# Attention stage: the row maximum from two GpSimd products and a VectorE maximum, instead of two clipped copies and three GpSimd instructions

## The reference, cut to what matters

```python
Q = (x @ Wq + bq).reshape(b, s, H, C) * inv_sqrt_c        # H = 16, C = 64
K = (x @ Wk + bk).reshape(b, s, H, C)
V = (x @ Wv + bv).reshape(b, s, H, C)
scores = jnp.einsum('bshq,bshk->bshqk', Q, K)             # an outer product per head
mask = jnp.triu(jnp.ones((C, C), dtype=bool), 1)
scores = jnp.where(mask, -jnp.inf, scores)
w = jax.nn.softmax(scores, axis=-1)
attn = jnp.einsum('bshqk,bshk->bshq', w, V)
out = attn.reshape(b, s, HID) @ Wo + bo
```

## Time and profile before

| what | value |
|---|---|
| median of the three runs | 3987.61 us |
| the profiled execution, its own time | 3990.44 us |
| its span in the profile | 3988.7 us |
| TensorE busy, share of the span | 3543.9 us, 89% |
| VectorE busy | 3277.2 us, 82% |
| ScalarE busy | 1974.6 us, 50% |
| GpSimd busy | 3341.5 us, 84% |
| L1249 (subtract, GpSimd), 768 instructions | 2509.0 us |
| chain that ended last, by engine | GpSimd 34%, TensorE 21%, issue 15%, VectorE 3% |

### The profile page before, as it was taken

One profiled execution on the slowest core, in us unless ns is written; L12 is line 12 of the kernel. 1 busy time (PEld: TensorE's weight loads), 2 busy tenths in 40 slices (PEclk: granted clock), 3 DMA queues, 4 the chain that ended last, 5 costly groups with the idle time before them and its releaser, 6 DMA issues.

```text
span 3988.7 us, 72222 instructions
## 1 busy us (share of the span) xinstructions
PE 3543.9 (89%) x25866; PEld 3108.7 (78%) x26059; DVE 3277.2 (82%) x3459; ACT 1974.6 (50%) x2535; POOL 3341.5 (84%) x1502
## 2 busy tenths in 40 slices
PE   5593699977699999999999999999999999999999
PEld 4252588866488888888888888888888888888888
DVE  8536555547699998899999999998999999999988
ACT  1010233344266655655555556555555555565555
POOL 1678455541699999999999999999999999999997
PEclk8696899998799999999999999999999999999999
DMA  9322456669000000000000000000000000000000
GB/s 381 109 101 80 140 178 197 187 210 339 14 5 5 8 5 5 5 5 5 5 5 6 6 5 8 5 5 5 5 5 6 5 5 6 5 8 5 5 5 5
DMA packets 110620, 209.18 MB, mean 52 GB/s; under 512 B 16608, under 2 KB 77280, under 8 KB 110304
## 3 DMA queue, kind: packets, MB, share of 16 engines
q1 hardware_dynamic: 84192, 140.90, 10.8%
q0 software_dynamic: 21504, 59.93, 4.1%
q10 hardware_dynamic: 4608, 4.20, 0.3%
HBM read 183.34 MB, written 107.74 MB: 73 GB/s over the span
## 4 chain that ended last, share of the span: by engine, by line
POOL 34%; PE 21%; issue 15%; DVE 3%; ACT 1%; another core or an unknown queue 0%; POOLq 0%; DVEq 0%; ACTq 0%
POOL at_s L1249 31%; PE at_num L1483 8%; PE at_den L1483 7%; PE at_work L1460 3%; PE at_work L1470 1%; POOL at_m L1234 1%; POOL at_fall L1231 1%; DVE at_pv L1167 1%; DVE at_k_low L1395 1%; PE at_misc L1515 1%; DVE at_s L1167 1%; PE at_misc L1509 1%; ACT at_s L1328 1%; DVE at_k_top L1392 0%; DVE at_pv L1168 0%
## 5 line engine op out<-in xcount | busy, mean ns | idle before, releaser
L1249 POOL TENSOR_TENSOR at_s<-at_s,at_m 128x2048 f32<-128x2048 f32 (+7 forms) x768 | 2509.0, 3303 | 34.9 <-DVE at_s L1167 25.4
L1328 ACT ACTIVATE at_s<-at_s 128x2048 f32<-128x2048 f32 (+7 forms) x768 | 1081.8, 1420 | 607.5 <-POOL at_s L1249 606.9
L1483 PE MATMUL at_den<-k_ident,at_s 128*128 128x128 f32 (+2 forms) x9216 | 1136.5, 273 | 50.3 <-ACT at_s L1328 50.3
L1483 PE MATMUL at_num<-k_ident,at_pv 128*128 128x128 f32 (+2 forms) x9216 | 1144.0, 274 | 14.0 <-issue 4.2
L1483 PEld LDWEIGHTS at_num<-k_ident,at_pv 128*128 128x128 f32 (+2 forms) x9216 | 1044.5, 141 | 90.7 <-issue 69.2
L1483 PEld LDWEIGHTS at_den<-k_ident,at_s 128*128 128x128 f32 (+2 forms) x9216 | 1031.8, 139 | 83.0 <-ACT at_s L1328 59.2
L1168 DVE TENSOR_TENSOR at_pv<-at_s,at_vp 128x2048 f32<-128x2048 f32 (+7 forms) x512 | 690.5, 1349 | 228.2 <-ACT at_vp L1303 174.6
L1168 DVE TENSOR_TENSOR at_s<-at_q,at_kp 128x2048 f32<-128x2048 f32 (+7 forms) x512 | 689.8, 1348 | 16.0 <-ACT at_kp L1298 11.2
L1167 DVE TENSOR_TENSOR at_pv<-at_s,at_vp 128x2048 f32<-128x2048 f32 x256 | 583.9, 2281 | 0.0
L1167 DVE TENSOR_TENSOR at_s<-at_q,at_kp 128x2048 f32<-128x2048 f32 x256 | 581.2, 2270 | 0.0
L1460 PE MATMUL at_work<-k_region,at_xT 128*128 128x512 f32 x788 | 409.8, 646 | 104.1 <-ACT at_k_far L1269 81.7
(11 more groups left out here) (235 smaller groups left out, 3475.6 us busy)
## 6 DMA issues: line engine op xcount, KB each, us to landing
moe_w<-experts SPq DMA_DIRECT2D x256, 384.0 KB
slot_x<-k_region SPq DMA_DIRECT2D x16, 2144.0 KB, 25.2
moe_x<-slot_x SPq DMA_DIRECT2D x256, 134.0 KB, 2.7
cmb_y<-picked SPq DMA_DIRECT2D x32, 768.0 KB, 7.7
at_xT<-xT SPq DMA_DIRECT2D x33, 128.0 KB, 2.1
e_x<-u SPq DMA_DIRECT2D x4, 1024.0 KB, 9.4
picked<-moe_yo,moe_row POOLq DMA_INDIRECT x256, 3.1
xT<-cmb_xT ACTq DMA_DIRECT2D x32, 128.0 KB, 5.9
```

Source lines behind the costliest of these rows:

```text
L1249: nc.gpsimd.tensor_tensor(part(s_slot, c), part(s_slot, c), by_query(m[unit_of(c)][:], c), ALU.subtract).then_inc(sub_done, 1)
L1328: nc.scalar.activation(part(s_slot, c), part(s_slot, c), ACT.Exp, scale=C ** -0.5).then_inc(exp_done, 1)
L1483: ins = nc.tensor.matmul(dst[0:wide, b * P:(b + 1) * P], buf[:, at:at + wide], k.ident[:], start=(c in (0, NTRI) and x == 0 and b == 0), s ...
```

## The change

`keep_q` now only copies q, and tells the others at once. GpSimd makes two products with q itself (`rise`): fall = k_low * q and m = k_top * q, behind its chunks 2 and 3 (unit 1) and behind chunks 20 and 21 (unit 0 of the next tile; the first of them stands ahead of `gated`). The third instruction goes to VectorE (`maxima`): m = max(m, fall), at its chunk 0 for unit 0 and at its chunk 6 for unit 1, behind that chunk's product, its `times_v` and its `divide`. Both inputs of this maximum lie in SBUF. The semaphore `max_step` becomes two, `risen` and `max_done`.

```diff
-                    if step == 0:
                         pool.wait_ge(scanned, t * 4 + 4)
                         pool.wait_ge(q_out, n + 1)
-                        nc.gpsimd.tensor_tensor(rows(m[h], FRONT), turned(k_top), rows(m[h], FRONT), ALU.mult).then_inc(max_step, 1)
-                    elif step == 1:
-                        nc.gpsimd.tensor_tensor(rows(fall), turned(k_low), rows(fall), ALU.mult).then_inc(max_step, 1)
+                        wait(pool, max_done, n)
+                        nc.gpsimd.tensor_tensor(rows(fall), turned(k_low), rows(q[h], FRONT), ALU.mult).then_inc(risen, 1)
                     else:
-                        pool.wait_ge(max_step, n * 3 + 2)
-                        nc.gpsimd.tensor_tensor(m[h][:, FRONT:QL], m[h][:, FRONT:QL], fall[:], ALU.subtract
-                                                ).then_inc(max_step, 1)
+                        wait(pool, sub_done, (t - 1) * NCH + (NCH if h else NTRI))
+                        nc.gpsimd.tensor_tensor(rows(m[h], FRONT), turned(k_top), rows(q[h], FRONT), ALU.mult).then_inc(risen, 1)
...
-                MAXIMA_HERE, MAXIMA_NEXT = {2: 0, 3: 1, 4: 2}, {21: 0, 22: 1, 23: 2}
+                RISE_HERE, RISE_NEXT = {2: 0, 3: 1}, {20: 0, 21: 1}
...
                         if c in (0, NTRI):
-                            pool.wait_ge(max_step, t * 6 + (3 + 3 * unit_of(c)))
+                            pool.wait_ge(max_done, t * 2 + (1 + unit_of(c)))
...
-                    nc.scalar.copy(q[h][:, FRONT:QL], work[:])
-                    wait(act, sub_done, past)
-                    nc.scalar.activation(m[h][:, FRONT:QL], work[:], ACT.Relu)
-                    wait(act, max_step, n * 3)
-                    nc.scalar.activation(fall[:], work[:], ACT.Relu, scale=-1.0).then_inc(q_out, 1)
+                    wait(act, risen, n * 2 - 2)
+                    nc.scalar.copy(q[h][:, FRONT:QL], work[:]).then_inc(q_out, 1)
...
-                        wait(dve, max_step, t * 6)
+                        wait(dve, risen, t * 4)
...
+                def maxima(t, h):
+                    n = t * 2 + h
+                    dve.wait_ge(risen, n * 2 + 2)
+                    v.tensor_tensor(m[h][:, FRONT:QL], m[h][:, FRONT:QL], fall[:], ALU.max).then_inc(max_done, 1)
...
+                MAXIMA_NEAR, MAXIMA_FAR = 0, 6
...
+                        if c == MAXIMA_NEAR:
+                            maxima(t, 0)
+                        if c == MAXIMA_FAR:
+                            maxima(t, 1)
```

More of the change, by code:

```diff
@@ L1099, in attention_and_ffn @@
         xT_in = [a.sem(f"xT_in{u}") for u in range(2)]
-        work_done, k_out, q_out, v_out, up_out, scanned, max_step = (
-            a.sem(s) for s in ("work_done", "k_out", "q_out", "v_out", "up_out", "scanned", "max_step"))
+        work_done, k_out, q_out, v_out, up_out, scanned, risen, max_done = (
+            a.sem(s) for s in ("work_done", "k_out", "q_out", "v_out", "up_out", "scanned", "risen", "max_done"))
         kp_ready, vp_ready, mult_done, sub_done, exp_done, pv_done = (
@@ L1220, in _, with rise @@
             def _(pool):
-                def maxima(t, h, step):
+                def rise(t, h, step):
                     n = t * 2 + h
@@ L1250, in tile @@
                                                 ALU.subtract).then_inc(sub_done, 1)
[L1251 to L1254, removed]
+                        if c in RISE_HERE:
+                            rise(t, 1, RISE_HERE[c])
+                        if c in RISE_NEXT:
+                            rise(t + 1, 0, RISE_NEXT[c])
                         if c == GATED:
                             gated(t)
-                for step in range(3):
-                    maxima(0, 0, step)
+                for step in range(2):
+                    rise(0, 0, step)
                 tile_loop(pool, tile)
```

## The result

| | kernel before | changed kernel |
|---|---|---|
| median of 20 runs each | 3987.64 us | 3995.23 us |
| lowest to highest | 3983.95 to 3992.97 | 3987.08 to 4009.30 |
| profiled execution, its own time | 3990.44 us | 4009.30 us |
| its span | 3988.7 us | 4007.5 us |

The ratio is 1.0019, 95% interval 1.0012 to 1.0027: 7.6 us slower, where +16 us was forecast. The sign was right, the size was not, and the changed kernel's runs spread over 22 us where those of before spread over 9. The profiled execution is the slowest of the 20, so I read its tiles one by one rather than its total.

The account below looks back on a forecast made before the run. A ring of waits through VectorE, TensorE and ScalarE was taken to bound the kernel. +0.39 us a tile gave +12 in 30 tiles, with +5 for the clock and -1 at the start +16: about 4004 us, range 3968 to 4020.

Parts of the forecast that it names:

- The ring of 42.04 + 47.33 + 2.45 us: Legs from VectorE's start to TensorE's V1, to ScalarE's copy of q, back to VectorE: the whole 91.82 us tile.
- GpSimd's 2.57 us of removed work: Two GpSimd instructions fewer a tile, outside the ring of waits: claimed to be worth nothing by itself.
- ScalarE, -0.96: Between the copy of Q1 and exp(1): without the two relus, vp comes 0.96 us earlier in the ring.
- VectorE, +0.60: The far maximum behind chunk 6 pushes VectorE's next instruction back by 0.60 us, covered by no idle time.
- The collision, +0.75: At the far maximum, VectorE waits 0.75 us for the rest of GpSimd's chunk 5 subtraction; chance 0.50.
- the main case: VectorE's far maximum waits only for the rest of GpSimd's running instruction: 3998 to 4016 us, chance 0.50.
- The ring, +0.39: Net change of the ring of waits, -0.96 + 0.60 + 0.75 = +0.39 us a tile, +12 us in 30 tiles.
- The clock, +5: TensorE's clock falls: if all 30 tiles pay 1.58 us instead of 24, +9 us; half taken, +5.
- the rival with chunk 6 ahead: GpSimd's chunk 6 goes ahead of the waiting far maximum, a 2.0 us wait: 3990 to 4037 us, chance 0.10.
- The sum: All terms together: +16 us on the profiled execution's 3990.44, so 4006.4, median about 4004; slower with chance 0.57.
- Second case (GpSimd lets VectorE in): The far maximum isn't held: -0.36 us a tile, faster, 3969 to 3977 us, chance 0.27.

Follow-up runs that it names:

- r4: The kernel before with VectorE's two K1 scans one chunk earlier, behind chunks 11 and 12: 3911.39 us, ratio 0.9805.
- r7: The changed kernel with two unread ScalarE relus put back behind each copy of q: 4007.29 us, ratio 1.0052.
- r1: The changed kernel timed and profiled again, unaltered: 3999.28 us, ratio 1.0035.
- r5: The kernel before plus an unread VectorE maximum behind chunks 0 and 6, one input in SBUF and one in PSUM: 3975.90 us, ratio 0.9971.
- r6: The kernel before plus an unread VectorE maximum behind chunks 0 and 6, both inputs in SBUF: 4010.62 us, ratio 1.0056.
- r8: The changed kernel with GpSimd's wait for the far maximum moved from chunk 8 to chunk 6: 3994.38 us, ratio 1.0020.
- r9: The kernel before plus two unread ScalarE relus behind the copy of K0 at chunk 7, delaying exp(8): 3947.18 us, ratio 0.9894.

## Why the prediction was right in its sign and wrong in its size

- **What bounds.** The ring of 42.04 + 47.33 + 2.45 us held: r4 and r7 moved it. GpSimd's 2.57 us of removed work turned into idle time, as said: it is busy for 86.5 us of a 92.2 us tile, where it was busy for 88.5 of 91.8. In r4 GpSimd bounds, by its busy time.
- **ScalarE, -0.96.** On the ring, by r7's direction, and about 1.05 us by the tiles of r7 and r1 that pay no fall.
- **VectorE, +0.60.** The next instruction is pushed back by 1.22 us, 0.60 without the hold; r5 has 0.68 us for the instruction itself, and its tiles that pay no fall are 0.5 us longer than 90.24.
- **GpSimd.** Forecast 3.0 us of waiting for Q0 and none for Q1; measured 3.05 and none in the tiles that pay a fall, and 1.6 us for Q0 in the others. The near maximum is held 0.62 us, where about a microsecond was forecast, off the ring.
- **The collision, +0.75.** 0.5 to 0.9 us in the 92.16 us tiles, 0.84 in the 90.7 ones, 1.8 to 2.1 in the 91.95 ones, where chunk 6 goes first. I had the last as a rival of its own, with a chance of 0.10; it came in 14 of 31 tiles of r1, in one execution with the main case. The mean hold in r1 is 2.01 - 0.69 = 1.32 us, so the term is 0.57 us a tile too small: 31 x 0.57 = 18 us. The Trainium skill ("SBUF — State Buffer", "Who interferes with whom") is borne out by r6 against r5. What it leaves open, and r8 shows, is that GpSimd's next instruction can get in ahead of the one that waits.
- **The ring, +0.39.** In tiles that pay the clock as before, 92.16 - 91.82 = +0.34: right. They are 21 of 31 tiles in the first profile and 8 in r1. With the mean hold the ring grows by -0.96 + 0.60 + 1.32 = +0.96 us a tile in r1, +30 us.
- **The clock, +5. This step failed.** "If a longer tile pays in all 30, it is 6 x 1.58 = +9 more. I take half." The bounds reached only from nothing to more falls paid; the runs show fewer. What lengthens the ring by the maximum lengthens TensorE's first wait too. In the first profile, r1 and r8 no fall came behind first waits of 1.65 to 1.75 us, and nearly all those tiles pay as before. Behind 1.9 us the clock fell in some of their tiles, and behind 2.9 us and more in all, and there the fall costs nothing. I had written that mechanism down under the rival with chunk 6 ahead, and not carried it into the main case. Measured in r1: 9 of 31 tiles pay instead of 25, and 16 x about 1.5 us (92.16 - 90.7) makes the term -24 us where I had +5.
- **The sum.** +30 - 24 = +6 us for r1's profiled execution, whose own time is 4.8 us above that of the kernel before; the 20 runs give +7.6. So +16 was an error of +18 us and one of -29 that mostly cancel, and that the result came as near as this is luck. The sign isn't luck alone: r8, where chunk 6 can't go first, is the case as I stepped it. It has a mean hold of 0.66 us and 24 paid falls, for which the sum without the clock's term is 31 x 0.30 = +9 us, and it measured +6.8. There the clock's term is about nothing.
- **Second case (GpSimd lets VectorE in).** It doesn't happen: no far maximum lasts less than 1.19 us. Its price wasn't tested. r5, a ring 0.60 us longer that gives 12 us back, shows that the length of the ring alone doesn't give the sign.

## What to carry to other kernels

When three engines are each nearly full, find the ring of waits that adds up to the period, and price an edit only by its part of that ring; then look at what the edit does to the idle times of TensorE, since the place of an idle time decides whether a fall of the clock is paid. A cheap VectorE instruction with both inputs in SBUF isn't cheap beside a GpSimd that streams from SBUF: its price is the rest of GpSimd's instruction, and perhaps the next one. And an engine that became lighter was worth nothing while another ring bounded. Breaking that ring, by moving the two scans of K1 a chunk ahead, gave 78 us to the kernel before and only 21 (25 against r1) to the changed one, whose maximum still collides.

## What the runs showed of the hardware that was not expected

- VectorE's 512-element maximum took 0.68 us in all 64 cases with one input in PSUM and 1.35 us in the median, up to 4.64, with both in SBUF (r5, r6). A waiting VectorE instruction isn't always first in line: in 14 of 31 tiles of r1 it lasted 2.5 to 2.8 us, because GpSimd's next 1.29 us subtraction went ahead; with GpSimd made to wait for it none lasted over 1.55 us behind the first tile (r8).
- Waits of TensorE of 1.9 to 2.4 us were followed by the clock at half speed in some tiles and not in others, with the same length of wait (r1, r5, r9); after 1.35 us it never was in the profiles of the kernel before.
- Two added ScalarE instructions a tile made the kernel 41 us faster (r9): of 25 falls of the clock that were paid, 14 came ahead of a wait instead and the others didn't come. In this kernel a fall's cost depends on what comes after it: 1.58 us behind the ring's last wait, nothing ahead of it.
